# Key parts kept in DRAM in the order of the stack, and their writes issued by GpSimd

## What is computed

```
layer 0: q = LoRA(x), k, v = LoRA(ctx)     # 8 key/value heads, each shared by 4 query heads
         x1 = x + LoRA_o(softmax(q k' / 4) v)
layer 1: Q = x1 Wq' + bq; K = ctx Wk' + bk; V = ctx Wv' + bv      # 32 key/value heads
         x2 = x1 + (softmax(mask(Q K' / 4)) V) Wo' + bo
         out = layernorm(x2) * ln_g + ln_b
LoRA(a) = a W + 2 (a A) B
```

## Time and profile before

| | us |
|---|---|
| median of 3 runs | 1662.81 (1661.9 to 1664.44) |
| profiled execution, its own time | 1668.17 |
| its span, first to last instruction | 1666.3 |
| PE busy | 1581.1 (95%) |
| DVE busy | 1216.4 (73%) |
| ACT busy | 1005.8 (60%) |
| POOL busy | 177.6 (11%) |
| DMA queue of SP | 47.1% of 16 engines' span, 165.48 MB |

### The profile page before, as it was taken

How to read it: one execution, slowest core, us unless ns; L and a number is a source line. 1 busy time by engine, 2 the same in 40 slices (tenths; PEclk the granted TensorE clock), 3 DMA queues, 4 the chain that set the end, 5 groups by cost and what they waited for, 6 DMA issues and landing times.

```text
span 1666.3 us, 42831 instructions
## 1 busy us (share of the span) xinstructions
PE 1581.1 (95%) x17828; PEld 1133.7 (68%) x17828; DVE 1216.4 (73%) x2669; ACT 1005.8 (60%) x1855; POOL 177.6 (11%) x274
## 2 busy tenths in 40 slices
PE   6899999999999999899989999999989999999997
PEld 3657666676666765655667777776767677777763
DVE  2667778677777777678867777588777778778782
ACT  0146666566666666576656666656656666666665
POOL 2000221001221011121211110000000001000000
PEclk8789999999999999999999999999999999999998
DMA  8645542534454233455436455634375346644520
GB/s 218 140 130 143 123 109 81 145 75 93 103 141 122 63 78 84 82 118 138 101 81 124 89 94 90 156 58 81 71 149 85 65 69 123 128 76 71 85 40 14
DMA packets 93970, 168.22 MB, mean 101 GB/s; under 512 B 21900, under 2 KB 70060, under 8 KB 93776
## 3 DMA queue, kind: packets, MB, share of 16 engines
q1 hardware_dynamic: 93776, 165.48, 47.1%
HBM read 114.62 MB, written 48.78 MB: 98 GB/s over the span
## 4 chain that ended last, share of the span: by engine, by line
PE 87%; issue 5%; DMA 2%; DVE 2%; SPq 1%; ACT 1%; POOL 0%; DVEq 0%; POOLq 0%
PE value L1093 23%; PE ring L1057 14%; PE work L1001 13%; PE work L1021 13%; PE score L1070 9%; PE score L1075 7%; PE work L1046 4%; PE work L1115 3%; DVE chunk_max L1240 1%; PE work L1029 1%; DMA m_dram<-m_turned 1%; ACT p_sb L1154 1%; PE work L984 1%; DMA ctx_sb<-ctxT 0%; SPq L1431 0%
## 5 line engine op out<-in xcount | busy, mean ns | idle before, releaser
L1240 DVE TENSOR_REDUCE chunk_max<-ring 128x1 f32<-128x402 f32 x2048 | 1046.0, 567 | 314.1 <-PE ring L1057 304.7
L1154 ACT ACTIVATE p_sb<-score 124x512 f32<-124x512 f32 (+1 forms) x1664 | 929.8, 597 | 546.7 <-PE score L1070 278.8
L1057 PE MATMUL ring<-k_stack,q_stack 64*128 64x402 f32 x2048 | 728.7, 448 | 42.4 <-issue 32.9
L1057 PEld LDWEIGHTS ring<-k_stack,q_stack 64*128 64x128 f32 x2048 | 339.9, 189 | 143.4 <-issue 64.1
L1093 PE MATMUL value<-p_sb,v_sb 124*32 124x256 f32 x6656 | 432.1, 388 | 1.6 <-issue 0.8
L1070 PE MATMUL score<-q_stack,k_stack 64*124 64x512 f32 (+1 forms) x832 | 365.4, 506 | 5.1 <-ACT p_sb L1154 3.3
L1075 PE MATMUL score<-q_stack,k_stack 64*124 64x256 f32 (+1 forms) x1664 | 344.2, 315 | 4.1 <-ACT p_sb L1154 2.0
L1021 PE MATMUL work<-wv,ctx_sb 64*124 64x128 f32 x3840 | 333.4, 276 | 4.8 <-issue 4.7
L1021 PEld LDWEIGHTS work<-wv,ctx_sb 64*124 64x124 f32 x3840 | 317.8, 187 | 9.0 <-issue 6.2
L1001 PE MATMUL work<-ctx_sb,wk 64*128 64x402 f32 x1280 | 295.7, 507 | 2.2 <-ACT full L1165 1.0
L1093 PEld LDWEIGHTS value<-p_sb,v_sb 124*32 124x32 f32 x6656 | 184.5, 110 | 161.0 <-issue 51.9
(11 more groups left out here) (64 smaller groups left out, 365.7 us busy)
## 6 DMA issues: line engine op xcount, KB each, us to landing
k_stack<-k_dram SPq DMA_DIRECT2D x288, 200.1 KB
k_dram<-k_parts SPq DMA_DIRECT2D x60, 402.0 KB, 3.2
ctx_sb<-ctxT SPq DMA_DIRECT2D x24, 992.0 KB, 12.2
q_stack<-q_dram SPq DMA_DIRECT2D x64, 256.0 KB, 3.7
q_dram<-q_parts SPq DMA_DIRECT2D x96, 128.0 KB
k_dram<-k_parts SPq DMA_DIRECT2D x20, 395.0 KB, 3.3
wq<-l_Wq SPq DMA_DIRECT2D x2, 1024.0 KB, 7.4
xt_sb<-xT SPq DMA_DIRECT2D x4, 512.0 KB, 11.6
```

Of the source, the lines that this page charges most:

```text
L1057: engine.matmul(ring[bank_of["max", u, half, m]][:, 0:MW], q_stack[rows, u % 3, j, q * P:(q + 1) * P], k_stack[rows, 2 * (z % 3) + (u % 2 ...
L1154: engine.activation(p_sb[0:tn, n % PLACES, :], score_bank[n % 2][0:tn, :], ACT.Exp, scale=SCALE).then_inc(s_exp, 1)
L1240: engine.tensor_reduce(chunk_max[:, u % 2, half, m // NM, m % NM:m % NM + 1], ring[bank_of["max", u, half, m]][:, 0:MW], AX.X, ALU.max)\
```

## The change

`k_dram` gets the order of the stack: sequence, block of 32 key columns, part (three, with the high part twice), column, key. The host code puts the columns of the key weights and of the key bias into a matching order. A stack is then loaded by two DMAs of 48 partitions with 12.8 KB on each, in place of six. The mask row is loaded for a stack of layer 1 only where its slot held another batch (12 of 32 stacks). Keys occupy rows 0 to 47 of a half, and the rows of ones, mask and maxima start at 48 (`XROW`), not 32.

The writes of keys and queries leave the list of steps: POOL issues three DMAs right behind its subtraction, for keys (each 201 KB) as for queries. The high part of the keys is thus written twice. The wait for the older loads of the queries moves to POOL with them.

In the plan, `stack` steps and unit entries no longer force pending writes out. In layer 0 the stack of an even unit is loaded one unit earlier (at the entry of odd unit u, for u+3), and the keys of the next batch fall due one unit earlier. The pair of maxima steps comes `late` and `late + 2` score steps after the collection, in place of 1 and 2.

```diff
-        if name[0] == "stack":
-            self.write_keys(None)
+    def write_later(self, after, *name):
+        self.writes.append((self.now + after, name))
+        self.writes.sort(key=lambda x: x[0])
...
+    def write_all(self, *kinds):
+        self.steps += [name for _, name in self.writes if name[0] in kinds]
+        self.writes = [x for x in self.writes if x[1][0] not in kinds]
...
-            self.writes += [(self.now + 1, ("write m", unit)), (self.now + 2, ("load m", unit))]
+            late = 1 + int(max(0.0, self.vector_free - max(self.free)) / 1800)
+            self.write_later(late, "write m", unit)
+            self.write_later(late + 2, "load m", unit)
...
-            todo += [(start + (UB - 2) * NT - 5, start + 2, ("k", b, g)) for g in k]
+            todo += [(start + (UB - 3) * NT - 5, start + 2, ("k", b, g)) for g in k]
...
+            if u % 2 and u + 3 < L0:
+                for g in range(self.NM // 2):
+                    self.ensure("k", self.seq_of(u + 3), g)
             self.ensure("q", (u + 2) // 2)
-            self.write_keys(None)
...
-        self.step("stack", u)
-        if u >= self.L0 or u % 2 == 0:
-            self.arrival = max(self.arrival, max(self.free) + 2000) + self.LOAD_STACK
-        self.stack_at[u] = self.arrival
+        early = (u + 1,) if u % 2 and u + 1 < self.L0 else ()
+        for n in (u,) + early:
+            if n in self.stack_at:
+                continue
+            if n >= self.L0 or n % 2 == 0:
+                self.step("stack", n)
+                self.arrival = max(self.arrival, max(self.free) + 2000) + self.LOAD_STACK
+                self.stack_at[n] = self.arrival
+            else:
+                self.stack_at[n] = self.stack_at[n - 1]
...
-    KPARTS = ((0, 0), (1, 1), (3, 0))
-    QPARTS = ((0, 0), (1, 0), (3, 1))
-    XROW = 2 * HD
+    KPARTS = ((0, 0), (1, 1), (2, 0))
+    QPARTS = ((0, 0), (1, 0), (2, 1))
+    XROW = 3 * HD
...
-        k_dram = nc.dram_tensor("k_dram", [5 * B, 2, P, T], F32R, kind="Internal").ap()
+        k_dram = nc.dram_tensor("k_dram", [5 * B, 4, 3, 2 * HD, T], F32R, kind="Internal").ap()
...
+    # GpSimd, "read k", behind the subtraction
+                    e.wait_ge(s_part, parts + 2)
+                    for r, part in KPARTS:
+                        engine.dma_start(raw(k_dram[seq, :, r, :, lo:hi]), raw(k_parts[:, n % 2, part, 0:hi - lo]))\
+                            .then_inc(s_kdw[n % 2], 16)
...
+    # GpSimd, "read q", behind the subtraction
+                    e.wait_ge(s_part, parts + 2)
+                    first = 2 * pair % 4
+                    for u in (2 * pair - 4, 2 * pair - 3):
+                        if u >= 0:
+                            e.wait_ge(s_q[u % 3], 16 * (u // 3 + 1))
+                    for r, part in QPARTS:
+                        engine.dma_start(raw(q_dram[first:first + 2, :, r, :, :])
+                                         .rearrange("u h d (j s) -> (u h) (d j) s", j=2),
+                                         raw(q_parts[:, pair % 2, part, :])).then_inc(s_qdw[pair % 2], 16)
...
-                elif kind == "write k":
-                elif kind == "write q":
...
-                    for r, part in KPARTS:
-                        keys = raw(k_dram[seq, part, row:row + count, :])
-                        for half in range(2):
...
-                    if u >= L0:
+                    for half in range(2):
+                        keys = k_dram[seq, block + (half if u >= L0 else 0)].rearrange("r (d j) t -> (r d) (j t)", j=2)
+                        engine.dma_start(
+                            raw(k_stack[64 * half:64 * half + XROW, 2 * g:2 * g + 2, :]).rearrange("p a t -> p (a t)"),
+                            raw(keys)).then_inc(s_kst[g], 16)
+                    if mask_changes(z):
```

More of the change, by code:

```diff
@@ L87, in step, with write_due @@
     def step(self, *name):
-        if name[0] == "stack":
-            self.write_keys(None)
         self.steps.append(name)
-    def write_keys(self, now):
-        while self.writes and (now is None or self.writes[0][0] <= now):
+    def write_later(self, after, *name):
+        self.writes.append((self.now + after, name))
+        self.writes.sort(key=lambda x: x[0])
+    def write_due(self, now):
+        while self.writes and self.writes[0][0] <= now:
             self.steps.append(self.writes.pop(0)[1])
+    def write_all(self, *kinds):
+        self.steps += [name for _, name in self.writes if name[0] in kinds]
+        self.writes = [x for x in self.writes if x[1][0] not in kinds]
     def tiles_of(self, name):
@@ L141, in read @@
                 self.step("read k", name[1], c)
-                self.writes.append((self.now + 3, ("write k", name[1], c)))
         elif kind == "v":
@@ L149, in read @@
             self.step("read q", name[1])
-            self.writes.append((self.now + 1, ("write q", name[1])))
         else:
@@ L563, in score @@
         self.budget += self.plan_rate() / 2
-        self.write_keys(s)
+        self.write_due(s)
         if self.next_stack is None and s % self.NT < 6:
@@ L726, in end @@
     def end(self):
-        self.write_keys(None)
+        self.write_all("write m", "load m")
         z = 2 * self.B - 1
@@ L813, in source, with batch_of, mask_changes @@
     def source(z):
-        return (z // 4, z % 4 * 2 * HD, 2 * HD) if z < L0 // 2 else \
-            (B + (z - L0 // 2) // 2, z % 2 * 4 * HD, 4 * HD)
+        return (z // 4, z % 4) if z < L0 // 2 else (B + (z - L0 // 2) // 2, z % 2 * 2)
+    def batch_of(z):
+        return (z - L0 // 2) // UB if z >= L0 // 2 else None
+    def mask_changes(z):
+        return z >= L0 // 2 and batch_of(z) != batch_of(z - 3)
     def max_window(c):
@@ L1538, in sync @@
                         e.wait_ge(s_kx[g], 32)
-                    for r, part in KPARTS:
-                        keys = raw(k_dram[seq, part, row:row + count, :])
-                        for half in range(2):
[L1543 to L1546, removed]
-                    if u >= L0:
-                        b = (u - L0) // UB
+                    for half in range(2):
[4 more added lines that the diff above has]
+                    if mask_changes(z):
+                        b = batch_of(z)
                         e.wait_ge(s_mask, 1)
@@ L1576, in sync @@
             for s, sem_k in enumerate(s_kdw):
-                e.wait_ge(sem_k, 16 * (plan.keys // 2))
+                e.wait_ge(sem_k, 16 * len(KPARTS) * (plan.keys // 2))
             e.wait_ge(s_out, 16 * rows)
@@ L1605 @@
         arrays[f"l1_W{n}"] = a[f"L1_xattn_W{n}"].T
-    arrays["l1_bk"] = a["L1_xattn_bk"].reshape(H // 128, 128).T
+    order = np.arange(128).reshape(4, 2, 16).transpose(0, 2, 1).reshape(128)
+    for n in ("l0_Wk", "l0_Bk"):
+        arrays[n] = arrays[n][:, order]
+    order = np.arange(H).reshape(H // 64, 2, 2, 16).transpose(0, 2, 3, 1).reshape(H)
+    arrays["l1_Wk"] = arrays["l1_Wk"][:, order]
+    arrays["l1_bk"] = a["L1_xattn_bk"][order].reshape(H // 128, 128).T
     order = np.arange(H).reshape(H // 64, 2, 2, 16).transpose(0, 2, 3, 1).reshape(H)
```

12 lines of the change are left out of this document (5 added, 7 removed).

## The result

The changed kernel takes 1797.5 us (median; 1786.2 to 1803.6) where the kernel before takes 1663.6 in the same comparison: a ratio of 1.0789, 95% interval 1.0724 to 1.0853. It is slower by 134 us. The forecast was 1627 with a range of 1602 to 1664; it was wrong in sign and far outside its range. The profiled execution of after is one of 1786.2 us, with a span of 1784.4.

A forecast was written before the change was run, and what follows sets the result against it. PE was taken as the bound, at 87% of the chain, with only its stands and low-clock time recoverable. Terms 24 + 19 - 3 - 2 - 2 = 36 us off 1662.8 gave 1627 us, range 1602 to 1664.

The forecast's parts named there:

- shape and size of the writes: New four-block key writes take 3.5 us a chunk, between 2.4 and 7.0, and stay hidden in layer 0.
- c: POOL's time to issue one write DMA, taken as 1.0 us, bounded by 0.36 and 2.7.
- Writes on POOL: Moving key and query writes to POOL: a key product costs it 9 us, not 3, hidden at 11.0 apart.
- rival 1: POOL becomes the bound in layer 0 from an issue cost of 2.5 us; about 1680 to 1774 us; chance 0.12.
- rival 2: Key writes stay on four engines, 7.0 us a chunk, delaying start and early layer 1 stacks; 1654 us; chance 0.14.
- the 6 kept back in layer 1: 6 us left at two places because layer 1's first four key sequences are just in time and their writes end later.
- Earlier stacks in layer 0: Loading stacks one unit ahead removes all six stands of the maxima and their clock loss; 24 us of 30 taken.
- Two loads for six: A stack's load to PE's resuming falls from 12.5 to 10 us; layer 1 gains 19 us.
- Maxima and plan: Mask-row loads behind a stack in SP's queue cost 2 us; new due times in PE's list cost 2 more.
- Start: Query writes and first stack at the kernel's start come later, with the first maximum possible around 50 us; costs 3 us.

The follow-up runs named there:

- e1_ring: Changed kernel with GpSimd's descriptor store at 8192 bytes a partition instead of 2048; 1668.7 us.
- e7_spread_m_ring: Changed kernel with key writes in 32 blocks, due mask rows ahead of query and stack loads in SP's list, and an 8192-byte descriptor store; 1615.3 us.
- e3_sp: Changed kernel with key and query writes issued by SP from its step list again, key writes still in 4 blocks; 1891.1 us.
- e9_four_m_ring: Changed kernel, key writes still in 4 blocks, with an 8192-byte descriptor store and due mask rows ahead of query and stack loads; 1653.9 us.
- e4_early: Kernel before with only the plan's part: keys due a unit earlier and layer 0's even-unit stacks loaded a unit earlier; 1641.8 us.
- e8_no_early: e6_spread_m with the plan's part undone: layer 0 stacks loaded and keys due as before; 1628.5 us.
- e6_spread_m: e2_spread with due mask rows put ahead of the loads of queries and stack in SP's list; 1615.3 us.
- e2_spread: Changed kernel with key columns reordered so key writes go in 32 blocks of 4 rows, store still 2048 bytes; 1639.1 us.

## Why the prediction was wrong

**The step that failed** is the one on shape and size of the writes: "I take 3.5. The two bounds make 5 to 14 us per key product against 11.0 apart, still hidden in layer 0". It treated a write's transfer as time that lies behind GpSimd. GpSimd's issue is tied to it: there was room for one group of three, so that the next had to wait for the transfer, and transfer, split and issue came in series instead of side by side. Then a chunk costs 0.5 + 1.0 + 2.1 + a stand of up to 11.4 us: the groups around 540 follow each other after 8.7 to 15.0 us, 17 or more for the two of a product, where products come every 11.0 us. ACT, in whose queue the exponentials stand, is held up. This had no term, no bound and no rival: c was bounded by the earlier trace rows, SP's issues, and the store that GpSimd's issues need did not appear in them. The program's own line that sizes it was there to be read. Cost: 129 us (after against e1_ring). Step by step, one edit each, the way from the best form (1615, e7_spread_m_ring) to the changed kernel is 39 us for the four blocks, 15 for mask rows behind other loads, and 129 for the small store.

**Writes on POOL, c.** 1.0 us taken, 0.70 measured (0.56 with 32 blocks). The size of c was right or better, and rival 1, which turned on c from 2.5, did not happen in the form it was given. Its symptom, ACT waiting for POOL, came all the same, by another price than the one it was made to hang on.

**Writes on four engines** (rival 2). The 7.0 us a chunk and the rate of 86 GB/s are near what e3_sp shows for SP: 92 GB/s, and some 14 us for two chunks. From GpSimd the writes overlap, but not to the 2.4 us of the forecast's lower bound: the landing of one write takes 5.6 to 6.7 us. Its price was 1654, with 11 us at the start. e9_four_m_ring, where only this cost is left beside the gains, measures 1653.9, and its first maximum comes at 60.9 us, 11 behind the 49.9 of before. The start is near what the rival had; that the totals agree is luck, since a price of 27 on 1627 meets one of 39 on the 1615 of the best form. That this was the smaller part of what four blocks do was missed. In the sum itself it stood as 3 at the start and within the 6 kept back in layer 1.

**Earlier stacks in layer 0.** 24 us taken, 20.9 measured by e4_early (interval of the ratio: 13 to 28). Right, in place too: all six stands went and the clock returned. On top of the other changes the same edit is worth 13 (e8_no_early against e6_spread_m), so the gains of the plan and of the shorter load do not simply add, as the sum had them.

**Two loads for six.** 12.5 us were to become 10; 11.1 and 10.3 were measured. No run has this term alone. e6_spread_m against e4_early gives 26.5 us for the layout, the issuer, the later maxima and the mask order together, where the sum had 19 - 3 - 2 - 2 = 12. The Trainium skill's rule on ports ("SBUF — State Buffer", "Door 1: The DMA port swizzle") would have had the transfer at 6 to 7.5 us. This case's traces allow it: in e2_spread 1.49 MB flow from 1126.0 to 1134.5 us at 175 GB/s, of which 1.23 MB are the stack and the rest the queries loaded just ahead, so the stack has some 7 us of it (an estimate by bytes). In e4_early, with six loads, 1.63 MB take 12 us from 1178 at 136 GB/s.

**Maxima and plan.** 2 us were taken for `load m` behind a stack. It was 23.6 in after (12.8 + 10.8) and 21.6 in e2_spread. The row of waits names it, and e6_spread_m against e2_spread removes it with 24 us. The mistake was to count "two or three waits of a us" by the stack's issue; what stood ahead in SP's queue was once a group of four context loads, whose issue took 12 to 13 us, and once the stack's 1.2 MB, behind whose transfer 4 KB of mask rows had to pass.

**Start.** +3 taken; in after the first maximum comes at 71.2 us, 21 later than before, by the same store: the query writes stand behind four groups of keys (with the large store it is 57.45, in e1_ring). In e2_spread it comes at 50.6.

**Range and chances.** Of the 0.15 for slower 0.12 hung on c, and the upper end of 1664 left that rival out; a stand of GpSimd at a small c had no chance of its own. With the key writes in 32 blocks the forecast of 1627 lies between e2_spread (1639) and e6_spread_m (1615). So the sum was near for that form, but partly by luck: it had 24 us for the earlier stacks, which beside the shorter load give 13, and 2 us against it for mask rows, which cost 24. It did not belong to this kernel.

## What to carry to other kernels

Before moving DMAs to GpSimd, count how many of them will be in flight at once and look at the program's store for their descriptors: here a small store made the issue as slow as the transfer, and it showed as "issue" ahead of a DMA and as waits of whoever needed GpSimd next. Look at the outermost dimension on both sides of a write: 32 in place of 4 was worth 158 us here with the small store, and 39 with the large one and the mask rows ahead. If the layout forbids it, the columns of the weights that produce the tensor can be reordered, as in e2_spread. When a step leaves or joins a queue in order, list what is issued between a small late load (here the mask rows) and its reader, loads of other tiles included.

## What the runs showed of the hardware that was not expected

- Stands of GpSimd ahead of its DMAs by the size of the store: 495 us at 2048 bytes, 57 at 4096, none at 8192, with the same DMAs; 11 at 2048 when the key writes are in 32 blocks (e2_spread).
- Six DMAs with four blocks in flight from SP keep the DMA share at 0.27 and 92 GB/s (over 12 us), as if on the same four engines; from GpSimd three of them reach 0.60 and 164 GB/s.
- An issue on GpSimd for 128 rows takes 0.70 us in 4 blocks and 0.56 in 32, both less than the subtraction over the same rows (1.0).
- From GpSimd the four-block form has 30720 more packets than the other, 128 for each of its 240 writes; from SP it has 2880 fewer. Why stays open, and with it how much of e2_spread's gain is packets and how much engines. From SP the 32 blocks give 253 us with more packets, so there it is not the packets.
